# Cross-attention key stacks: all copies written to memory, then one load over 128 partitions

## What is computed

```python
q_c = _ln(x) @ W_qc + b_qc
kv_c = _ln(context) @ W_kvc + b_kvc
k_c, v_c = jnp.split(kv_c, 2, axis=-1)
# 16 heads of width 8
c_attn_w = jax.nn.softmax(jnp.einsum('bhqd,bhsd->bhqs', q_c, k_c) * scale, axis=-1)
c_attn_out = jnp.einsum('bhqs,bhsd->bhqd', c_attn_w, v_c)
```

## Time and profile before

| what | value |
|---|---|
| time, median of 3 runs | 8284.53 us (8252.77 to 8294.11) |
| time of the profiled execution | 8326.02 us |
| its span, first to last instruction | 8324.2 us |
| mean granted TensorE clock | 0.691 of 2.4 GHz |
| TensorE matmul busy | 5950.0 us (71%) |
| VectorE busy | 4418.3 us (53%) |
| ScalarE busy | 3049.7 us (37%) |
| transfers, all queues | 563.09 MB, mean 68 GB/s |

### The profile page before, as it was taken

How to read it: one execution, slowest core, us unless ns; L and a number is a source line. 1 busy time by engine, 2 the same in 40 slices (tenths; PEclk the granted TensorE clock), 3 DMA queues, 4 the chain that set the end, 5 groups by cost and what they waited for, 6 DMA issues and landing times. The chain is left out here.

```text
span 8324.2 us, 193086 instructions
## 1 busy us (share of the span) xinstructions
PE 5950.0 (71%) x73102; PEld 3970.2 (48%) x73102; DVE 4418.3 (53%) x7950; ACT 3049.7 (37%) x4356; POOL 1592.6 (19%) x866
## 2 busy tenths in 40 slices
PE   4638677777875747778778876789464777777787
PEld 3415455454543525455555544555342555555554
DVE  5536566555664435555555653323553555655555
ACT  2214444444542214344444442213231344444444
POOL 2043222222312022121112200000212121212210
PEclk6656677767766556777677767769555677777767
DMA  3255555555512255555555501110325646555550
GB/s 74 62 79 79 78 73 81 76 78 79 80 26 48 79 81 82 77 74 82 78 78 82 77 14 43 46 36 0 73 55 84 87 70 87 79 79 79 78 78 14
DMA packets 453049, 563.09 MB, mean 68 GB/s; under 512 B 119994, under 2 KB 402394, under 8 KB 442970
## 3 DMA queue, kind: packets, MB, share of 16 engines
q1 hardware_dynamic: 452186, 551.01, 42.2%
HBM read 379.45 MB, written 169.54 MB: 66 GB/s over the span
## 5 line engine op out<-in xcount | busy, mean ns | idle before, releaser
L1215 DVE TENSOR_REDUCE maxima<-ps 100x1 f32<-100x482 f32 (+1 forms) x4608 | 2750.0, 650 | 2263.4 <-PE ps L1047 2059.9
L1170 ACT ACTIVATE probs<-ps 128x800 f32<-128x800 f32 (+1 forms) x2304 | 1810.2, 834 | 2370.9 <-PE ps L1074 2364.0
L1047 PE MATMUL ps<-kst,qst 48*100 48x482 bf16 (+1 forms) x4608 | 1883.8, 517 | 639.3 <-DVE maxima L1215 504.8
L1092 PE MATMUL ps<-probs,vals 128*9 128x100 f32 x36864 | 1381.7, 305 | 251.7 <-issue 250.6
L1074 PE MATMUL ps<-qst,kst 51*128 51x100 bf16 x18432 | 1456.1, 243 | 124.3 <-issue 119.0
L1092 PEld LDWEIGHTS ps<-probs,vals 128*9 128x9 f32 x36864 | 976.7, 108 | 693.9 <-issue 460.2
L1074 PEld LDWEIGHTS ps<-qst,kst 51*128 51x128 bf16 x18432 | 1100.3, 116 | 308.9 <-issue 212.0
L1268 POOL TENSOR_TENSOR kparts<-kf,zero 128x1444 bf16<-128x1444 f32 x192 | 497.7, 2592 | 3762.0 <-ACT kf L1142 3740.5
L1047 PEld LDWEIGHTS ps<-kst,qst 48*100 48x100 bf16 x4608 | 634.9, 143 | 1130.2 <-DVE maxima L1215 803.8
L1019 PE MATMUL ps<-ident,ctok 128*128 128x128 f32 (+1 forms) x1152 | 224.0, 326 | 332.7 <-issue 122.5
L1024 PE MATMUL ps<-ctxT,perm_wk_L 128*128 128x512 f32 (+1 forms) x576 | 326.0, 680 | 44.5 <-DVE maxima L1215 27.8
(11 more groups left out here) (253 smaller groups left out, 5696.3 us busy)
## 6 DMA issues: line engine op xcount, KB each, us to landing
ctx_k_parts<-kparts SPq DMA_DIRECT2D x192, 541.5 KB
kst<-ctx_k_parts SPq DMA_DIRECT2D x192, 541.5 KB
kst<-ctx_k_parts SPq DMA_DIRECT2D x192, 361.0 KB
ctok<-in_ctx_dram SPq DMA_DIRECT2D x96, 704.0 KB
kst<-ctx_k_parts SPq DMA_DIRECT2D x192, 180.5 KB
c<-in_ctx_dram SPq DMA_DIRECT2D x32, 704.0 KB
o_self_sums<-osb SPq DMA_DIRECT2D x24, 800.0 KB
o_sums<-osb SPq DMA_DIRECT2D x96, 200.0 KB
```

What stands on the lines that cost most here:

```text
L1047: nc.tensor.matmul(ps[0:N, at:at + w], g.qst[s][row0:row0 + CROWS, j, :], g.kst[s][row0:row0 + CROWS, j, a:a + w], start=True, stop=True). ...
L1092: ins = nc.tensor.matmul(ps[q:q + VW, o:o + N], vals[s][:, kt, h, :], probs[kt % 2][hf][:, CH * e + N * jj:CH * e + N * jj + N], start=(kt ...
L1170: nc.scalar.activation(probs[kt % 2][hf][0:kts[kt], :].rearrange("p (k n) -> p k n", k=2), src, ACT.Exp).then_inc(exp_done, 1)
L1215: nc.vector.reduce_max(maxima[:, col:col + 1], ps[0:N, at:at + widths[c]], AX.X).then_inc(m_read, 1)
```

## The change

The buffer in memory takes the form of the whole stack: 128 rows of 8 heads x 1,444 columns, with every copy in it, and the 16 rows of ones in each half, written once in L0. `sp_keys_out` writes six transfers in place of two: first parts 0, 1 and 2 into slots 0 to 2, then parts 0 and 1 into slots 3 and 4, then part 0 into slot 5, each transfer for one half (64 partitions outermost). `sp_stacks` loads the key stack by one transfer over 128 partitions, and the query stack by six in place of 12, with the copies of a part made by a broadcast source. In L0, VectorE sets `kst[0]` to ones and SyncE writes its rows of ones to the three buffers before the first slot; the memsets of the stacks in L1 and L3, and GpSimd's in L0, are left out.

```diff
+    K_RUNS = ((0, 3), (3, 2), (5, 1))
+    KW = 16 * 2 * len(K_RUNS)
+    Q_SLOTS = ((0, 3), (3, 2), (5, 1))
...
+        def slot_rows(s, e, first, n):
+            return g.kscr[s].rearrange("(e r d) (j n) -> e (d j) r n", e=2, d=HD, j=PAIRS)[e, :, first:first + n]
...
-                wait(g.pe, k_loaded[s], 16 * 6 * (r + 1))
-                wait(g.pe, qst_loaded[s], 16 * 12 * (r + 1))
+                wait(g.pe, k_loaded[s], 16 * (r + 1))
+                wait(g.pe, qst_loaded[s], 16 * 6 * (r + 1))
...
-            wait(pool, k_written[p.s], 16 * 2 * (p.r + 1))
+            wait(pool, k_written[p.s], KW * (p.r + 1))
...
-            wait(sp, k_written[s], 16 * 2 * (r + 1))
-            rows = [g.kscr[s][e].rearrange("t (d j) n -> (t d) (j n)", j=PAIRS) for e in range(2)]
-            for first, end, src in ((0, 24, 0), (24, 40, 0), (40, 48, 0)):
-                for e in range(2):
-                    sp.dma_start(g.kst[s][HALF * e + first:HALF * e + end, :, :].rearrange("p j n -> p (j n)"),
-                                 rows[e][src:src + end - first, :]).then_inc(k_loaded[s], 16)
-            for slot, part in enumerate(SLOT_Q):
-                for e in range(2):
-                    at = HALF * e + HD * slot
-                    sp.dma_start(g.qst[s][at:at + HD, :, :].rearrange("p j n -> p (j n)"),
-                                 g.qx[bass.ds(b, 1), e, part].rearrange("a (d j) n -> (a d) (j n)", j=PAIRS)).then_inc(qst_loaded[s], 16)
+            wait(sp, k_written[s], KW * (r + 1))
+            sp.dma_start(g.kst[s][:, :, :].rearrange("p j n -> p (j n)"), g.kscr[s]).then_inc(k_loaded[s], 16)
+            for e in range(2):
+                for part, (first, copies) in enumerate(Q_SLOTS):
+                    at = HALF * e + HD * first
+                    sp.dma_start(g.qst[s][at:at + HD * copies, :, :].rearrange("p j n -> p (j n)"),
+                                 g.qx[bass.ds(b, 1), e, part].rearrange("a (d j) n -> a d (j n)", j=PAIRS)
+                                 .to_broadcast([copies, HD, PAIRS * N])).then_inc(qst_loaded[s], 16)
...
-            for e in range(2):
-                sp.dma_start(g.kscr[s][e].rearrange("t r n -> r t n"), parts[HALF * e:HALF * e + HALF, :, :]).then_inc(k_written[s], 16)
+            for first, n in K_RUNS:
+                for e in range(2):
+                    sp.dma_start(slot_rows(s, e, first, n), parts[HALF * e:HALF * e + HALF, 0:n, :]).then_inc(k_written[s], 16)
...
-                nc.vector.memset(g.kst[0][:, :, :].rearrange("p j n -> p (j n)").bitcast(F32), ONE_PAIR).then_inc(stacks_set, 1)
+                if normed:
+                    nc.vector.memset(g.kst[0][:, :, :].rearrange("p j n -> p (j n)").bitcast(F32), ONE_PAIR).then_inc(stacks_set, 1)
...
-                for s in range(1, LAG):
-                    nc.gpsimd.memset(g.kst[s][:, :, :].rearrange("p j n -> p (j n)").bitcast(F32), ONE_PAIR).then_inc(stacks_set, 1)
...
+                if normed:
+                    sp.wait_ge(stacks_set, 1)
+                    for s in range(LAG):
+                        for e in range(2):
+                            rows = slice(HALF * e + CROWS, HALF * e + HALF)
+                            sp.dma_start(g.kscr[s][rows, :], g.kst[0][rows, :, :].rearrange("p j n -> p (j n)")).then_inc(ones_written, 16)
+                    sp.wait_ge(ones_written, 16 * 2 * LAG)
                 for b in range(-3, 1):
-                    if b == -2:
-                        sp.wait_ge(stacks_set, LAG)
                     sp_slot(known(b))
...
-    g.kscr = [nc.dram_tensor(f"ctx_k_parts{s}", (2, PARTS, HALF, S), BF16).ap() for s in range(LAG)]
+    g.kscr = [nc.dram_tensor(f"ctx_k_stack{s}", (P, PAIRS * S), BF16).ap() for s in range(LAG)]
```

More of the change, by code:

```diff
@@ L972, in cross_attention_phase @@
         ones, zeros, ctx_std, stacks_set = sem("ones"), sem("zeros"), sem("ctx_std"), sem("stacks_set")
+        ones_written = sem("ones_written")
         set_up = 1 + 2 * LAG
+        def slot_rows(s, e, first, n):
+            return g.kscr[s].rearrange("(e r d) (j n) -> e (d j) r n", e=2, d=HD, j=PAIRS)[e, :, first:first + n]
         def max_tile(slot, x):
```

## The result

| what | before | after |
|---|---|---|
| median of 4 runs, same chip | 8289.32 us (8252.77 to 8319.61) | 7553.73 us (7544.26 to 7562.27) |
| ratio, 95% interval | | 0.9114 (0.9075 to 0.9153) |
| profiled execution, its span | 8326.02, 8324.2 us | 7550.31, 7548.5 us |
| mean granted TensorE clock | 0.691 | 0.724 |
| transfers | 563.09 MB | 742.71 MB |

The change makes the kernel 8.9% faster. The forecast of 7700 us was 1.9% too high, inside its range.

A forecast was written before the change was run, and what follows sets the result against it. The prediction took TensorE's gaps, instruction fetches held up behind the slow key-stack load, as the cost to remove. 8326 - 558 (gaps) - 27 (starts) = 7741 us, by the factor 0.995 given as 7700; range 7480 to 8130.

The forecast's parts named there:

- The gaps are held-up fetches, beside the load: TensorE after the key-stack load's issue: instruction fetches wait behind key rows; 6.6 of 9.2 us a slot are idle time.
- The load, 9.5 us (8.1 to 26.4): Key-stack load in one transfer of 128 rows, 2.96 MB: 9.5 us, where the old load took about 24.
- the rival that it doesn't spread: Key-stack load still takes some 26 us, or the gaps have another cause: 8285 us, chance 0.06.
- "I take 35%" of the 9.2 us to stay: Cross-attention slots: 35% of the time above 50.3 us stays (bounds 13% and 60%); 6.0 us gained in 93 slots, 558.
- The loop's jump, 0.9 us a slot: TensorE at the hardware loop's jump: a 2.7 us gap once in three slots, perhaps unrelated to the load, 10% staying.
- The writes, 10.4 us in place of 5.2, hidden: SyncE's key writes at each slot's start: 2.22 MB at 214 GB/s, 5.2 us later, covered by waits and an earlier reply.
- The query stack, 2.4 us of issue saved, 2.5 us of delay: SyncE's query-stack load: six issues for 12 save 2.4 us, the broadcast source delays the sums' reply 2.5 us, both hidden.
- "The stack itself is used a slot later.": Key stack: first used one slot after its load, given among reasons why the later writes cost nothing.
- the third rival: SyncE's queue becomes the bound: slots of 63.5 us against 59.5, so 8650 us, chance 0.10.
- Starts, -27: TensorE's wait for each phase's first load: 14 us less, the write before it 5.2 more; -9 us, three times.
- From profile to median, 0.995: Factor from the profiled execution, 8326.0 us, to the median, 8284.5; it turns 7741 us into 7703, given as 7700.
- The range: Whole kernel: bounds 7555 and 7957 us, or 7517 and 7917 as medians, widened to 7480 and 8130.

The follow-up runs named there:

- e10: Kernel before, with two SyncE waits between the three groups of its key-stack load: 7446.23 us, ratio 0.9096 to the kernel before.
- e11: Kernel before, with one SyncE wait after all six key-stack loads: 8103.43 us, ratio 0.9759 to the kernel before.
- e2: Changed kernel, key stack loaded by two transfers of 64 adjacent partitions: 7683.26 us, ratio 0.9245 to the kernel before.
- e4: Changed kernel, key stack loaded by eight transfers of 16 partitions standing eight apart: 7659.97 us, ratio 0.9216 to the kernel before.
- e1: Changed kernel, key stack loaded by the old six transfers, stacks set to ones as before: 8294.46 us, ratio 0.9984 to the kernel before.
- e6: Changed kernel, with the old 12 query-stack transfers: 7552.57 us, ratio 0.9083 to the kernel before.
- e9: Changed kernel, key stack loaded by eight transfers of 16 adjacent partitions, with waits before the fourth and seventh: 8300.77 us, ratio 1.0131 to the kernel before.

## Why the prediction was right, and where it was off

- **The gaps are held-up fetches, beside the load.** Right, and now shown by e10 and e11 and by the count of late blocks, where the prediction only had both at once. But it took the slower load and its rows to be what counts, and gave the gain to the rate. The rate is one way to a short queue; two waits are another.
- **The load, 9.5 us (8.1 to 26.4).** Right in kind, and 0.6 us below its lower bound: 7.5 us at 395 GB/s, in a window with the DMA share at 1.02. The reason, partitions reached, is shown by e2 to e4. Of the rival that it doesn't spread nothing is left.
- **"I take 35%" of the 9.2 us to stay.** This is the term that was off. The mean slot of the earlier trace rows's kind is now 50.9, so 0.6 us stay above 50.3, 6%, below the lower bound of 13%. The bound went wrong because it scaled the waits with the load's length; they fall much faster than that (e2: a load 0.64 as long, and idle time 0.31 of before). In the sum, 8.0 us for 87 slots and 40 us behind the last loads are 734, against 558.
- **The loop's jump, 0.9 us a slot.** Right in size: 87.2 us over 93 slots. But it doesn't come on top of 50.3: the mean slot of L1 is 50.3 us with its jumps in it, so slots without one are shorter than that.
- **The clock.** 2.0 of the 8.7 us a slot are the higher clock (mean 0.691 to 0.724), near the 2.6 us that the prediction gave to slower matmuls.
- **The writes, 10.4 us in place of 5.2, hidden.** Right. The six issues take 8.6 us (1.4 each, not 0.66), the window has 241 GB/s, and L1329 comes 11.3 us after the first L1352 (12.4 forecast). e1 shows that all this costs nothing. The cover named was right too: the reply came 16.8 us sooner (14 forecast), and the wait before L1344 grew from 10.5 to 14.1 us.
- **The query stack, 2.4 us of issue saved, 2.5 us of delay.** Neither can be seen. Six issues take 4.56 us where 12 took 4.84, so 0.76 each: almost nothing is saved. e6 shows no difference in the time, and a reply 0.5 us sooner. The Trainium skill's rule on a leading broadcast ("DMA: Bandwidth & Descriptors", Rules for kernel authors), which keeps such a transfer on few engines, isn't refuted by that, since a delay of that size would be hidden as well.
- **"The stack itself is used a slot later."** Wrong, as e9 showed: the first third of its row maxima is made in the same slot. It did no harm, because the load became shorter. In the third rival, with a load of 30 us, it could have mattered: TensorE would have waited too, as in e9.
- **Starts, -27.** -41 by the intervals, -37 by the wait for the first load (92.9 to 55.6). Writing the rows of ones in L0 costs 0.6 us at most: the first load is issued at 518.93 us, against 518.36 before.
- **From profile to median, 0.995.** The changed kernel's profiled run (7550.3) lies at its median; the factor took 41 us off a forecast of 7741 that was 190 us too high for the profiled run.
- **The range.** The profiled 7550.3 lies 5 us below the sum's own lower bound of 7555. The stated range reaches lower only by that factor, which didn't apply, and by what was added for the clock. So the mechanism was right, but the gain lay at the edge of what was argued, and that it fell inside the range is in part luck.

The sum therefore misses by 734 - 558 = 176 for the gaps and 41 - 27 = 14 for the starts: 7741 - 190 = 7551, the profiled 7550.3.

**Not settled.** On which transfer engine a fetch stands, what decides how large a part of the queue it waits for, and where between 15.6 and 24 us the idle time rises, no run shows. That fetches are asked for ahead, so that a delay below the lead stays hidden, would give this shape; it is only argued. Why e11 gains a quarter isn't shown either: it has 423 us of late fetches in place of 528, and the query and context rows that no longer queue behind the load are my guess at the reason. That e9's "issue" waits in L1100 halve but don't vanish (2.3 us each), with pieces of 9 us, is unexplained.

## What to carry to other kernels

Where an engine idles with "issue" as the end, beside a long transfer, look for instruction fetches behind it: first try waits inside the load that keep each queued piece to some 10 us (e10's largest is 11.6), which costs two lines here, and see whether what is loaded is still in time. Load and write over all 128 partitions in one transfer; if it must be a part, spread it over them (16 rows eight apart are as fast as 64 neighbours, and 1.7 times as fast as 16 neighbours). Before pricing a delay of a transfer, find its first reader in the code, not the phase that it is named for.

## What the hardware showed that I had not expected

**Small VectorE operations that take twelve times as long.** The negated row maximum is split into its bf16 parts by operations of 16 x 100 elements, one of which subtracts the first part. In the kernel before, its group by form (min/median/max ns, first and last start):

```profile
L1236 DVE TENSOR_TENSOR negmax<-negmax,nparts x96: 249/3006/3011, 591.3 to 8164.8; 16x100 f32<-16x100 f32 x96
```

The fastest takes 0.25 us, the median 3.0. In the timeline of the changed kernel it starts together with a GpSimd operation and ends with it:

```profile
1137.40 2.92 POOL L1305 TENSOR_TENSOR kparts<-kf,kparts 128x1444 bf16<-128x1444 f32 x1
1137.42 3.01 DVE L1244 TENSOR_TENSOR negmax<-negmax,nparts 16x100 f32<-16x100 f32 x1
...
1141.57 0.64 PE L1055 MATMUL ps<-kst,qst 48*100 48x482 bf16 x1 [4.25 <-DVE maxima L1223]
```

Over all 96 of the changed kernel it is the same: the 90 that take 3.0 us start some 0.02 us after that GpSimd operation and end some 0.11 us after it ends, and the six that take 0.25 us overlap no GpSimd operation. In the kernel before the split is 78 and 18. Behind the one shown TensorE has a gap of 4.25 us, waiting for VectorE's next maxima. The Trainium skill ("SBUF — State Buffer", SBUF: two separate sides) describes a pair of SBUF ports that VectorE and GpSimd share, held by one for a whole instruction; the 96 operations agree with it. That this gap would go if the two operations were kept apart was not tried. If all that the 96 take above 0.25 us each came back (their busy time is 272.2 us), that would be an estimated 248 us, more than anything left in the loads; it is an upper bound, since VectorE is not always what TensorE waits for.

**Issue times.** Both new forms take SyncE longer to issue. Median of one issue over the whole trace: the key write 1.35 us in its new form, 0.64 us before; the query load 0.68 us with the broadcast source, 0.28 us before, and 0.29 us in e6, where it stands behind the wide load too.
